# h stored whole and split in the third stage, reciprocal halves taken earlier, edge tiles placed earlier: a graph layer kernel on one core

## The chip, the cores and the metric

The kernel runs on one core of a Trainium2 chip. Its time is the device time of one launch in microseconds (us): a median of three runs, and beside it one execution that the hardware profiler recorded. The engines are TensorE (PE, its weight loads PEld), VectorE (DVE), ScalarE (ACT), GpSimd (POOL), and SyncE (SP), which here only issues transfers.

## The reference, cut to what matters

```python
def sage(x, W_l, W_r, b):                       # both layers use the same edges
    summed = segment_sum(x[src], dst, 10000)    # 10000 edges, 512 columns
    agg = summed / maximum(deg, 1)[:, None]
    return agg @ W_l.T + x @ W_r.T + b
xn = layernorm(x)                               # x: 10000 x 512
h = tanh(sage(xn, W1_l, W1_r, b1))
x = x + sage(h, W2_l, W2_r, b2) + linear_attention(xn)   # 8 heads, 64 features each
x = x + top1_of_8_experts(layernorm(x))
```

The linear attention needs, for each node and head, the query features times one shared matrix, divided by a denominator (the features times the sum of the keys' features). All matrix products are done as three products of halves: every operand is split into a high part, rounded to fp32r, and a low part, the full value minus the high one.

## The kernel before

The nodes are padded to 20 groups of 4 tiles of 128 nodes, 80 tiles. There are four stages, and each engine runs its own instruction stream; semaphores alone order them. The streams are written as loops over "steps": a function is called with `turn, k` for step t = 8 turn + k, and it works on tile t minus a lag that differs from one operation to the next (`active(t, lag, NT)`).

Stage 1 normalises the nodes and sums the keys. Stage 2 (`hidden`) computes h group by group: DVE adds the root part (`low`, L1031), ACT takes tanh and casts the high half (L836), DVE subtracts for the low half (`hT_made_low`), PE multiplies the halves with W2_l into y. SP loads the next group's `r_in` and `b_agg`, stores both halves of h to DRAM (L556) and y to `y_d`.

Stage 3 (`mix`) has one step for each tile. In step t:

- PE: in each fourth step the denominators of a group (L1315, 8 matmuls), then one matmul that spreads the inverse denominators of tile t-2 over its features (L1326), two matmuls that sum an edge tile (L417, L418), and 24 matmuls (L1200) for tile t-8, 12 of them with `hT_high` and `hT_low`, 12 with `qz_high` and `qz_low`.
- DVE: query features times the spread inverse of tile t-3 (`low<-phi_q,bank`, L1043), the build of one edge tile (`Sj`, `S`, `cnt`, `eidx`, L397 to L406), the addition of the product of tile t-9 to x (`m_x`, L1053), the low half `qz_low` of tile t-4; in each fourth step the reciprocal of the denominators (L1063), and in the step after it that reciprocal's low half (`z_halves`).
- ACT: the high half of the edge sources (`G_high`), in each fourth step that of the reciprocal (`z_halves`, L849), that of qz, and the copy of an edge sum to `O`.
- POOL: the low half of edge sources (`G_low`), the gather of an edge tile from `y_d` (L361), and the scatter of another (L378), which adds the rows `O` to `agg_d` in DRAM. The scatters are a chain: each waits until the one before it has landed (L377), since two could touch one row. The build of edge tile i waits until the scatter of tile i-4 has landed, and so does, by way of `G_low` behind the scatter in POOL's stream, the sum of tile i.
- SP: for each group the two halves of h (L593), the edge lists (L354), the store of a finished part (`part_d`, L597), x (`m_x`, L601) and query features (`phi_q`, L605), 1 MB each but for the lists.

An edge tile goes through its own steps s: gather at s, build and split at s+2, sum at s+3, scatter at s+4. The table `mix_edges` sets which s are done in which t: before, none for t below 6 and one in each step from there on, so that s = t-6, and the last sum is in step 88, one step after the last product (step 87). Stage 4 (`ffn`) begins when all scatters have landed: SP loads `agg2_g[0]` and `part_d[0]`, DVE makes x, its statistics and the normalised rows of four tiles, and PE transposes them (L1207).

Of the kernel before, what the change touches and what calls it, by code (L numbers as in the profile page):

```python
# [19 lines left out]
EDGE_FROM, EDGE_EXTRA = 6, 32  # L20
# [70 lines left out]
def build(nc, x, src, dst, w1lT, w1rT, b1, w2lT, w2rT, b2, wqT, wkT, wv, pmat, wproj, bproj,  # L91
          wr, br, f1, fb1, f2, fb2, ident_in, tri_in, bmask_in, hmask_in, trash_in, expand_in,
          iota_in, out):
    with ExitStack() as ctx:
# [9 lines left out]
        hT_d = split_d("hT", [NG, P, KC * GROUP])  # L104
        w1l_d, w2r_d, f1_d, f2_d = (split_d(w, [P, KC * D]) for w in ("w1l", "w2r", "f1", "f2"))
        q_d = nc.dram_tensor("q_d", [NG, P, KC * GROUP], F32)
# [66 lines left out]
        mhT = [at("hT_high", 2, 2, F32R), at("hT_low", 16, 2, F32R)]  # L173
# [98 lines left out]
        m_den, m_z, m_zh, m_zl, m_zb = (sem(f"mix_{n}") for n in ("den", "z", "z_high", "z_low", "z_spread"))  # L272
        m_qz, m_qh, m_ql = sem("mix_qz"), sem("mix_qz_high"), sem("mix_qz_low")
# [51 lines left out]
        for t in range(32):  # L325
            now = 0 if t < EDGE_FROM else 1 + (t % 2 if EDGE_EXTRA <= t < 32 else 0)
            mix_edges.append([(s // 8, s % 8) for s in range(done, done + now)])
            done += now
# [136 lines left out]
        def _(sp):  # L465
# [80 lines left out]
            def hidden(turn, b):  # L546
                g = 2 * turn + b
                end = isinstance(g, int) and g == NG
                if active(g, 1, NG):
                    sp.wait_ge(b_hl, 4 * g)  # L550
                    if end:
                        sp.dma_start(flat(phq[1]), q_d[1]).then_inc(m_ph[1], 16)
                    if active(g, -1, NG):
                        hid_in(*lagged(turn, b, -1, 2))
                    for n in range(2):
                        sp.dma_start(hT_d[n][g - 1], flat(bhT[n])).then_inc(b_hst, 16)  # L556
                    if end:
                        sp.wait_ge(b_hst, 64)
                        for i in range(2):
                            for n in range(2):  # L560
                                sp.dma_start(flat(mhT[n], i), hT_d[n][i]).then_inc(m_ht[i], 16)
                        for i in range(2):
                            edge_load(sp, 1, 0, i)
                    sp.wait_ge(b_yo, 4 * g)
                    sp.dma_start(y_g[g - 1], flat(by, 1 - b)).then_inc(b_yst[1 - b], 16)
                if isinstance(g, int) and g == 2:
                    sp.wait_ge(c_ml, KC)
                    for n in range(2):
                        sp.dma_start(flat(W2r[n]), w2r_d[n][:]).then_inc(s_w2r, 16)
                if isinstance(g, int) and g == 3:  # L570
                    sp.dma_start(flat(phq[0]), q_d[0]).then_inc(m_ph[0], 16)
# [6 lines left out]
            sp.wait_ge(b_hst, 32 * NG)  # L578
# [6 lines left out]
            def mix(turn, k):  # L585
# [3 lines left out]
                if active(g, 1, NG) and j == 0 and not (first and g < 3):  # L589
                    turn1, b1_ = lagged(turn, b, 1, 2)  # L590
                    sp.wait_ge(m_p, 4 * (g - 2))
                    for n in range(2):
                        sp.dma_start(flat(mhT[n], b1_), hT_d[n][g - 1]).then_inc(m_ht[b1_], 16)  # L593
# [54 lines left out]
        def _(pool):  # L648
# [67 lines left out]
            turns(pool, mix, 11, head=4, last=1)  # L716
# [14 lines left out]
        def _(act):  # L731
# [82 lines left out]
            def hidden(turn, b):  # L814
# [12 lines left out]
                if active(g, 0, NG):  # L827
                    for o in range(KC):
# [3 lines left out]
                        if o == 0:  # L832
                            need(act, b_y, 4 * g)
                            need(act, b_hst, 32 * g)
# [5 lines left out]
            def mix(turn, k):  # L840
                t = 8 * turn + k
                edges = edge_steps(turn, k)
                for te in edges[0:1]:
                    edge_high(act, 1, *te)
                if active(t, 1, NT) and k % 4 == 1:
                    g = 2 * turn + k // 4
                    act.wait_ge(m_z, g + 1)
                    need(act, m_zb, 4 * g)
                    act.copy(zs[0:STACK, :], pd[0:STACK, :]).then_inc(m_zh, 1)  # L849
                if active(t, 3, NT):  # L850
# [3 lines left out]
                    act.copy(mqz[0][:, kk // 4, kk % 4, :], low[:, kk % 4, :]).then_inc(m_qh, 1)  # L854
                for te in edges[0:1]:
# [18 lines left out]
            turns(act, mix, 11, head=4, last=1, skip=5)  # L874
# [31 lines left out]
        def _(dve):  # L906
# [104 lines left out]
            def hidden(turn, b):  # L1011
# [15 lines left out]
                for o in range(KC):  # L1027
                    if o == 0:
                        dve.wait_ge(b_rin[b], 16 * (turn + 1))
                    dve.wait_ge(b_h, 4 * g + o + 1)  # L1030
# [5 lines left out]
            group_turns(dve, hidden, 0, head=2, last=1)  # L1036

            def mix(turn, k):
                t = 8 * turn + k
                if active(t, 3, NT):  # L1040
# [13 lines left out]
                if active(t, 4, NT):  # L1054
# [3 lines left out]
                             mqz[0][:, kk // 4, kk % 4, :]).then_inc(m_ql, 1)  # L1058
                if active(t, 0, NT) and k % 4 == 0:
# [4 lines left out]
                if active(t, 1, NT) and k % 4 == 1:  # L1064
                    g = 2 * turn + k // 4
                    dve.wait_ge(m_zh, g + 1)
                    low_half(dve, zs[LOW:STACK, :], pd[LOW:STACK, :], zs[LOW:STACK, :]).then_inc(m_zl, 1)
# [6 lines left out]
            turns(dve, mix, 11, head=4, last=1)  # L1074
# [104 lines left out]
        def _(pe):  # L1179
# [164 lines left out]
            def mix(turn, k):  # L1344
# [8 lines left out]
                if active(t, 8, NT):  # L1353
                    turn8, kk = lagged(turn, k, 8)
                    b8, j8 = kk // 4, kk % 4
                    if j8 == 0:
                        pe.wait_ge(m_ht[b8], 32 * (turn8 + 1))
# [11 lines left out]
            turns(pe, mix, 11, head=4, last=1, skip=6)  # L1369
# [121 lines left out]
```

## Time and profile before

| | before |
|---|---|
| median of three runs | 2760.31 us (2755.53 to 2762.66) |
| profiled execution | 2753.52 us, span 2751.7 us |
| PE busy in the span | 2612.7 us |
| DVE busy | 1805.8 us |
| POOL busy | 1068.0 us |
| stage 2, from the first to the last group | about 1019 to 1491 us of the span |
| stage 3, steps with an edge sum | 1530.75 to 2131.87 us |
| first transpose of stage 4 | 2163.83 us |

Times inside the span count from its start. Busy time of PE is that of pipelined matmuls, whose ends are modelled; the start of one to the start of the next is the better measure of pace. Spans on POOL are rough. "Idle 4.85 <-DMA agg_d" behind an instruction says that its engine stood still for 4.85 us and what ended that.

### The profile page before, as it was taken

The numbers are of one execution on the slowest core, as the hardware profiler recorded it, in microseconds if no ns is written. First come the engines' busy times: TensorE is split into PE (matmuls) and PEld (weight loads), VectorE is DVE, ScalarE is ACT, GpSimd is POOL, SyncE is SP. The second block draws the span as 40 slices with busy tenths as digits, with TensorE's granted clock in tenths as the row PEclk, the third lists the DMA queues.
The fourth block names the chain that finished last, engine by engine and source line by source line (L and its number), as shares of the span: only waits on it lengthen the run. The fifth ranks groups of instructions, "written<-read, shape, count | busy, mean of one in ns | idle before, by whom it ended". The sixth has DMA issues, their size and how long they took to land.

```text
span 2751.7 us, 35957 instructions
## 1 busy us (share of the span) xinstructions
PE 2612.7 (95%) x11712; PEld 2084.5 (76%) x11712; DVE 1805.8 (66%) x3628; ACT 990.4 (36%) x1725; POOL 1068.0 (39%) x1009
## 2 busy tenths in 40 slices
PE   5999999999999989999999999999999499999999
PEld 4788888888888868888886666776667377777777
DVE  5577777777777734444444567777775577777774
ACT  3455454444444424444443222222222123233232
POOL 5677776666666620000000545455555211111110
PEclk8999999999999999999999999999999799999999
DMA  9766675555555446665556688887886423232231
GB/s 368 241 178 195 171 203 143 146 126 145 141 135 148 122 147 250 232 220 217 223 222 244 186 267 238 252 260 231 249 252 160 164 103 127 92 133 96 100 129 46
DMA packets 140315, 502.52 MB, mean 183 GB/s; under 512 B 27288, under 2 KB 27800, under 8 KB 99776
## 3 DMA queue, kind: packets, MB, share of 16 engines
q1 hardware_dynamic: 104384, 417.15, 41.7%
q0 software_dynamic: 35840, 84.23, 16.4%
q8 instruction: 47, 0.77, 0.1%
q14 instruction: 44, 0.36, 0.0%
HBM read 261.60 MB, written 239.73 MB: 182 GB/s over the span
## 4 chain that ended last, share of the span: by engine, by line
PE 72%; DMA 17%; DVE 4%; issue 3%; SPq 2%; ACT 1%; POOL 1%; POOLq 0%; DVEq 0%; ACTq 0%
PE bank L1200 56%; DMA agg_d<-O,eidx 14%; PE bank L1251 8%; PE bank L1207 3%; DVE x2T_low L314 2%; PE bank L1415 1%; SPq L484 1%; PE bank L417 1%; PE bank L418 1%; PE bank L1315 1%; ACT f_relu L883 1%; DVE f_relu L1119 1%; PE bank L1383 1%; PE bank L1400 0%; DMA a_x<-in_x 0%
## 5 line engine op out<-in xcount | busy, mean ns | idle before, releaser
L378 POOL DMA_INDIRECT agg_d<-O,eidx x160 | 271.6, 1697 | 300.9 <-DMA agg_d<-O,eidx 218.3
L314 POOL TENSOR_TENSOR G_low<-G,G_high 128x512 fp32r<-128x512 f32 x160 | 253.7, 1585 | 169.3 <-ACT G_high L439 169.2
L361 POOL DMA_INDIRECT G<-y_d,esrc x80 | 96.4, 1205 | 527.4 <-DMA y_d<-b_y 514.3
L397 DVE SCALAR_TENSOR_TENSOR Sj<-erow,dstf,tri 128x128 f32<-128x128 int32 x160 | 154.9, 968 | 146.6 <-DMA agg_d<-O,eidx 138.4
L439 ACT CAST G_high<-G 128x512 fp32r<-128x512 f32 x160 | 99.4, 621 | 315.6 <-DVE G L957 173.2
L723 POOL TENSOR_SCALAR veps<-mv 128x1 f32<-128x1 f32 x80 | 26.9, 337 | 472.9 <-DVE mv L1092 472.9
L314 DVE TENSOR_TENSOR qz_low<-low,qz_high 128x512 fp32r<-128x512 f32 x80 | 171.1, 2138 | 0.1
L406 DVE SCALAR_TENSOR_TENSOR eidx<-cnt,todump,dstf 128x1 int32<-128x1 f32 x160 | 149.7, 936 | 7.6
L688 POOL TENSOR_TENSOR pd<-pd,low 128x512 f32<-128x512 f32 (+1 forms) x80 | 143.3, 1792 | 0.0
L314 POOL TENSOR_TENSOR a_xn_rows_low<-a_x,a_xn_rows_high 128x512 fp32r<-128x512 f32 x80 | 142.9, 1786 | 0.2 <-ACT a_xn_rows_high L752 0.2
L1031 DVE TENSOR_TENSOR low<-bank,r_in 128x512 f32<-128x512 f32 x80 | 55.3, 692 | 131.0 <-PE bank L1200 131.0
L1200 PE MATMUL bank<-Wk_high,xnT_high 128*128 128x512 f32 x320 | 128.6, 402 | 6.3 <-DVE xnT_low L314 6.3
L1200 PE MATMUL bank<-xnT_high,W1r_high 128*128 128x512 f32 x320 | 131.5, 411 | 0.0
L1200 PE MATMUL bank<-W2r_high,hT_high 128*128 128x512 f32 x320 | 131.1, 410 | 0.0
L1200 PE MATMUL bank<-W2r_low,hT_high 128*128 128x512 f32 x320 | 130.5, 408 | 0.0
L966 DVE SCALAR_TENSOR_TENSOR low<-bank,low 128x512 f32<-128x512 f32 x80 | 55.3, 692 | 113.5 <-ACT low L770 113.5
L314 DVE TENSOR_TENSOR a_phi_low<-low,a_phi_high 128x512 fp32r<-128x512 f32 x80 | 59.9, 749 | 105.8 <-ACT a_phi_high L747 100.2
L1200 PE MATMUL bank<-W2r_high,hT_low 128*128 128x512 f32 x320 | 129.0, 403 | 0.0
L854 ACT CAST qz_high<-low 128x512 fp32r<-128x512 f32 x80 | 49.5, 619 | 218.2 <-PE bank L1200 148.0
L1200 PE MATMUL bank<-Wk_low,xnT_high 128*128 128x512 f32 x320 | 127.8, 399 | 0.0
L1200 PE MATMUL bank<-xnT_high,Wq_high 128*128 128x512 f32 x320 | 124.7, 390 | 2.5 <-DVE xnT_low L314 1.5
L1200 PE MATMUL bank<-Wk_high,xnT_low 128*128 128x512 f32 x320 | 127.0, 397 | 0.0
(199 smaller groups left out, 7872.0 us busy)
## 6 DMA issues: line engine op xcount, KB each, us to landing
agg_d<-zero SPq DMA_DIRECT2D x20, 1040.0 KB, 20.3
b_agg<-agg_d SPq DMA_DIRECT2D x20, 1040.0 KB, 8.5
a_x<-in_x SPq DMA_DIRECT2D x20, 1024.0 KB
agg_d<-z_halves SPq DMA_DIRECT2D x20, 1024.0 KB
q_d<-q_rows SPq DMA_DIRECT2D x80, 256.0 KB
r_d<-r_rows SPq DMA_DIRECT2D x80, 256.0 KB
r_in<-r_d SPq DMA_DIRECT2D x20, 1024.0 KB, 4.8
hT_high_d<-hT_made_high SPq DMA_DIRECT2D x20, 1024.0 KB, 10.4
```

Source lines behind the costliest of these rows:

```text
L314: return eng.tensor_tensor(out_, full, high.bitcast(F32), ALU.subtract)
L361: pool.indirect_dma_start(G[:, j, :], None, table, bass.IndirectOffsetOnAxis(ap=esrc[:, b, j:j + 1], axis=0)).then_inc(e_g[j], 16)
L378: pool.indirect_dma_start(agg, bass.IndirectOffsetOnAxis(ap=eidx[:, j, 0:1], axis=0), O[:, j, 0:width], None, compute_op=ALU.add).then_inc ...
L397: dve.scalar_tensor_tensor(Sj[:, :], row, dstf[:, b, j:j + 1], tri[:, :], ALU.is_equal, ALU.mult, accum_out=cnt[:, j:j + 1]).then_inc(e_cn ...
L406: dve.scalar_tensor_tensor(eidx[:, j, :], cnt1[:, j:j + 1], todump[:, b, j:j + 1], dstf[:, b, j:j + 1], ALU.mult, ALU.add).then_inc(e_s, 1)
L439: act.copy(G_high[:, j % 2, :], G[:, j, :]).then_inc(e_gh, 1)
L688: pool.tensor_tensor(acc[0:rows, :], acc[0:rows, :], low[0:rows, k % 4, :], ALU.add).then_inc(a_ks, 1)
L966: dve.scalar_tensor_tensor(lo, bank[7][:, :], 0.0, lo, ALU.max, ALU.add).then_inc(a_phi, 1)
L1031: dve.tensor_tensor(low[:, o, :], bank[2 + o % 2][:, :], rin[:, b, o, :], ALU.add).then_inc(b_hs, 1)
L1200: last = pe.matmul(out_, lhs(l, c), rhs(r, c), start=start and c == 0 and i == 0, stop=stop and c == KC - 1 and i == 2)
L1207: last = pe.transpose(psum[:, c * P:(c + 1) * P], row[:, c * P:(c + 1) * P], ident[:, :])
L1251: last = pe.matmul(bank[c][:, :], axr[l][:, 0, k5 % 4, c * P:(c + 1) * P], aph[r][:, k5 % 2, :], start=first and i == 0, stop=final and i ...
```

## The change

1. h is stored once, whole (1 MB a group instead of 2), from DVE's and ACT's working buffer `low`; this store is issued ahead of the loads of the next group. In stage 3 it is loaded once (1 MB instead of 2) into the place of `hT_low`; ACT then casts the high half and DVE subtracts for the low half, tile by tile, in step t for tile t-4, four steps ahead of the product. The load is still issued when the product of the group three back has been done, for its place is that of the old low half.
2. The reciprocal's high half on ACT now stands ahead of the high half of the edge sources, and its low half on DVE stands first in its step instead of last.
3. In steps 11, 15, 19, 23, 27 and 31 two edge tiles are done, the second behind the product. From step 32 on s = t: the last sum is in step 82, the last scatter in step 83.
4. The edge sources' low half stays on POOL (`edge_low` is not touched).

```diff
-EDGE_FROM, EDGE_EXTRA = 6, 32
...
-        hT_d = split_d("hT", [NG, P, KC * GROUP])
+        hT_d = nc.dram_tensor("hT_d", [NG, P, KC * GROUP], F32)
...
-        mhT = [at("hT_high", 2, 2, F32R), at("hT_low", 16, 2, F32R)]
+        mhT, hT = [at("hT_high", 16, 2, F32R), at("hT_low", 2, 2, F32R)], at("hT", 2, 2)
...
-            now = 0 if t < EDGE_FROM else 1 + (t % 2 if EDGE_EXTRA <= t < 32 else 0)
+            now = 0 if t < 6 else 1 + (t >= 8 and t % 4 == 3)
...
                     sp.wait_ge(b_hl, 4 * g)
+                    sp.dma_start(hT_d[g - 1], low[:, :, :].rearrange("p c n -> p (c n)")).then_inc(b_hst, 16)
                     if end:
                         sp.dma_start(flat(phq[1]), q_d[1]).then_inc(m_ph[1], 16)
                     if active(g, -1, NG):
                         hid_in(*lagged(turn, b, -1, 2))
-                    for n in range(2):
-                        sp.dma_start(hT_d[n][g - 1], flat(bhT[n])).then_inc(b_hst, 16)
...
                     sp.wait_ge(m_p, 4 * (g - 2))
-                    for n in range(2):
-                        sp.dma_start(flat(mhT[n], b1_), hT_d[n][g - 1]).then_inc(m_ht[b1_], 16)
+                    sp.dma_start(flat(hT, b1_), hT_d[g - 1]).then_inc(m_ht[b1_], 16)
...
-                for te in edges[0:1]:
-                    edge_high(act, 1, *te)
                 if active(t, 1, NT) and k % 4 == 1:
...
                     act.copy(zs[0:STACK, :], pd[0:STACK, :]).then_inc(m_zh, 1)
+                for te in edges[0:1]:
+                    edge_high(act, 1, *te)
...
+                if active(t, 4, NT):
+                    turn4, kk = lagged(turn, k, 4)
+                    if kk % 4 == 0:
+                        act.wait_ge(m_ht[kk // 4], 16 * (turn4 + 1))
+                    act.copy(mhT[0][:, kk // 4, kk % 4, :], hT[:, kk // 4, kk % 4, :]).then_inc(m_hh, 1)
...
                         dve.wait_ge(b_rin[b], 16 * (turn + 1))
+                        need(dve, b_hst, 16 * g)
...
+                if active(t, 1, NT) and k % 4 == 1:
+                    g = 2 * turn + k // 4
+                    dve.wait_ge(m_zh, g + 1)
+                    low_half(dve, zs[LOW:STACK, :], pd[LOW:STACK, :], zs[LOW:STACK, :]).then_inc(m_zl, 1)
...
+                    dve.wait_ge(m_hh, t - 3)
+                    low_half(dve, mhT[1][:, kk // 4, kk % 4, :], hT[:, kk // 4, kk % 4, :],
+                             mhT[0][:, kk // 4, kk % 4, :]).then_inc(m_hl, 1)
...
-                        pe.wait_ge(m_ht[b8], 32 * (turn8 + 1))
+                        pe.wait_ge(m_hl, t - 8 + 4)
```

DVE's stream in stage 3 of the program before, from the end of the step that takes a reciprocal into the step after it (`m_x` is the addition of a product, `low<-phi_q,bank` the query features times the spread inverse, the four rows between them the build of an edge tile):

```order
L1053 TENSOR_TENSOR m_x<-bank,m_x 128x512 [waits mix_product]
L314 TENSOR_TENSOR qz_low<-low,qz_high 128x512 [waits mix_qz_high]
L1063 RECIPROCAL pd<-bank 40x512 [waits mix_z_low,mix_den]
L1043 TENSOR_TENSOR low<-phi_q_96,bank 128x512 [waits mix_z_spread]
L397 SCALAR_TENSOR_TENSOR Sj,cnt<-erow,dstf,tri 128x128 [waits edge_scattered,edge_summed]
L399 TENSOR_SCALAR S,O<-erow,dstf 128x128
L402 TENSOR_SCALAR cnt<-cnt 128x1 [waits edge_repeats]
L406 SCALAR_TENSOR_TENSOR eidx<-cnt,todump,dstf 128x1 [waits edge_repeated]
L1053 TENSOR_TENSOR m_x<-bank,m_x 128x512 [waits mix_product,mix_x_in1]
L314 TENSOR_TENSOR qz_low<-low,qz_high 128x512 [waits mix_qz_high]
L314 TENSOR_TENSOR z_halves<-pd,z_halves 8x512 [waits mix_z_high]
```

The same place of the changed program:

```order
L1060 TENSOR_TENSOR m_x<-bank,m_x 128x512 [waits mix_product]
L314 TENSOR_TENSOR qz_low<-low,qz_high 128x512 [waits mix_qz_high]
L314 TENSOR_TENSOR hT_low<-hT,hT_high 128x512 [waits mix_h_high]
L1073 RECIPROCAL pd<-bank 40x512 [waits mix_z_low,mix_den]
L314 TENSOR_TENSOR z_halves<-pd,z_halves 8x512 [waits mix_z_high]
L1050 TENSOR_TENSOR low<-phi_q_97,bank 128x512 [waits mix_z_spread]
L397 SCALAR_TENSOR_TENSOR Sj,cnt<-erow,dstf,tri 128x128 [waits edge_scattered,edge_summed]
L399 TENSOR_SCALAR S,O<-erow,dstf 128x128
L402 TENSOR_SCALAR cnt<-cnt 128x1 [waits edge_repeats]
L406 SCALAR_TENSOR_TENSOR eidx<-cnt,todump,dstf 128x1 [waits edge_repeated]
L1060 TENSOR_TENSOR m_x<-bank,m_x 128x512 [waits mix_product]
```

Behind `qz_low` there is a new `hT_low` that waits for ACT, and the reciprocal stands behind it; the reciprocal's low half has moved from the end of the next step to its head.

SP's stream where stage 2 takes up its second and third group, before:

```order
L537 DMA r_in<-r_d 128x2048 [waits hid_h_low]
L538 DMA b_agg<-agg_d 128x2080
L556 DMA hT_high_d<-hT_made_high 128x2048
L556 DMA hT_low_d<-hT_made_low 128x2048
L565 DMA y_d<-b_y 128x2048 [waits hid_y_out]
```

and in the changed program:

```order
L551 DMA hT_d<-low 128x2048 [waits hid_h_low]
L537 DMA r_in<-r_d 128x2048
L538 DMA b_agg<-agg_d 128x2080
L563 DMA y_d<-b_y 128x2048 [waits hid_y_out]
L551 DMA hT_d<-low 128x2048 [waits hid_h_low]
```

One store now stands ahead of the two loads where two stores stood behind them.

## Rows read from the trace of the kernel before

**Rows 1.** Source line L378, 1490 to 2165 us: durations in ns, first and last start
```profile
L378 POOL DMA_INDIRECT agg_d<-O,eidx x80: 1552/1592/2097, 1539.5 to 2143.0; - x80
```

**Rows 2.** The chain that ended last: start us, us, what
```profile
1927.73 8.36 DMA agg_d<-O,eidx
1936.93 4.93 DMA agg_d<-O,eidx
1942.70 9.01 DMA agg_d<-O,eidx
1952.53 4.94 DMA agg_d<-O,eidx
```

**Rows 3.** Timeline of PE: the denominators of four groups, start us, us
```profile
1550.93 3.63 PE L1315 MATMUL bank<-phi_q,KS 128*40 128x512 f32 x8
...
1834.62 3.63 PE L1315 MATMUL bank<-phi_q,KS 128*40 128x512 f32 x8
1863.09 3.63 PE L1315 MATMUL bank<-phi_q,KS 128*40 128x512 f32 x8
...
2051.03 3.20 PE L1315 MATMUL bank<-phi_q,KS 128*40 128x512 f32 x7
```

**Rows 4.** What PE waited for, 1490 to 2165 us: us, times, longest
```profile
PE bank L1207 <- DVE f_xn L1098: 32.0, 1, 32.0
PE bank L1326 <- DVE z_halves L314: 22.7, 11, 3.8
PE bank L417 <- POOL G_low L314: 12.1, 5, 5.0
```

**Rows 5.** Timeline of SP: transfers that it issued in stage 3
```profile
1834.87 0.33 SPq L593 DMA_DIRECT2D hT_high<-hT_high_d  x1
...
1838.04 0.35 SPq L597 DMA_DIRECT2D part_d<-m_x  x1
...
2094.01 0.33 SPq L601 DMA_DIRECT2D m_x<-in_x  x1
```

**Rows 6.** Timeline of POOL: two scatters in a row late in stage 3
```profile
2096.72 1.59 POOL L378 DMA_INDIRECT agg_d<-O,eidx  x1 [1.43 <-ACT O L427]
...
2104.25 1.59 POOL L378 DMA_INDIRECT agg_d<-O,eidx  x1 [3.17 <-DMA agg_d<-O,eidx]
```

**Rows 7.** The DMA view, issues of stage 2: KB each, median us to landing
```profile
hT_high_d<-hT_made_high SPq DMA_DIRECT2D x18, 1024.0 KB, 10.4
hT_low_d<-hT_made_low SPq DMA_DIRECT2D x18, 1024.0 KB, 12.3
```

**Rows 8.** Timeline of DVE in stage 2, one group
```profile
1260.73 0.17 DVE L1002 TENSOR_SCALAR rd<-b_agg 128x4 f32<-128x4 f32 x1 [6.66 <-DMA b_agg<-agg_d]
...
1264.30 0.69 DVE L1031 TENSOR_TENSOR low<-bank,r_in 128x512 f32<-128x512 f32 x1 [1.30 <-PE bank L1200]
```

**Rows 9.** Timeline of the engines in stage 3: DVE and POOL side by side
```profile
1937.84 2.56 DVE L314 TENSOR_TENSOR qz_low<-low,qz_high 128x512 fp32r<-128x512 f32 x1
1937.98 1.86 POOL L314 TENSOR_TENSOR G_low<-G,G_high 128x512 fp32r<-128x512 f32 x1
1940.43 0.68 DVE L314 TENSOR_TENSOR z_halves<-pd,z_halves 8x512 fp32r<-8x512 f32 x1
```

**Rows 10.** Windows of stage 3: length, busy us of PE, PEld, DVE, ACT, POOL; clock, DMA share
```profile
1900.00:2000.00 100.00, 93.77 (x369) 69.01 (x369) 79.64 (x131) 24.00 (x43) 54.04 (x39) 0.97 0.83 242
```

**Rows 11.** From stage 3 to stage 4: first the chain, then DVE's timeline
```profile
2143.03 4.75 DMA agg_d<-O,eidx
2148.21 8.38 DMA f_x<-part_d
...
2156.61 0.17 DVE L1085 COPY rd<-rdeg 128x4 f32<-128x4 f32 x1 [24.49 <-DMA f_x<-part_d]
```

**Rows 12.** Timeline of PE: the last sum of stage 3, the first transposes of stage 4
```profile
2131.23 0.40 PE L417 MATMUL bank<-G_high,S 128*128 128x512 f32 x1
2163.83 2.58 PE L1207 MATMUL bank<-ident,f_xn 128*128 128x128 f32 x11 [31.96 <-DVE f_xn L1098]
```

More of the change, by code:

```diff
@@ L272, in build @@
         m_den, m_z, m_zh, m_zl, m_zb = (sem(f"mix_{n}") for n in ("den", "z", "z_high", "z_low", "z_spread"))
+        m_hh, m_hl = sem("mix_h_high"), sem("mix_h_low")
         m_qz, m_qh, m_ql = sem("mix_qz"), sem("mix_qz_high"), sem("mix_qz_low")
@@ L554, in hidden @@
                         hid_in(*lagged(turn, b, -1, 2))
-                    for n in range(2):
-                        sp.dma_start(hT_d[n][g - 1], flat(bhT[n])).then_inc(b_hst, 16)
                     if end:
-                        sp.wait_ge(b_hst, 64)
+                        sp.wait_ge(b_hst, 32)
                         for i in range(2):
-                            for n in range(2):
-                                sp.dma_start(flat(mhT[n], i), hT_d[n][i]).then_inc(m_ht[i], 16)
+                            sp.dma_start(flat(hT, i), hT_d[i]).then_inc(m_ht[i], 16)
                         for i in range(2):
@@ L577, in _ @@
                 sp.dma_start(flat(mx_, b), x_g[b]).then_inc(m_x[b], 16)
-            sp.wait_ge(b_hst, 32 * NG)
+            sp.wait_ge(b_hst, 16 * NG)
             sp.dma_start(craw[:, 0, 0:KC * EXP].rearrange("p (c e) -> p c e", c=KC), kpn(wr)
@@ L591, in mix @@
                     sp.wait_ge(m_p, 4 * (g - 2))
-                    for n in range(2):
-                        sp.dma_start(flat(mhT[n], b1_), hT_d[n][g - 1]).then_inc(m_ht[b1_], 16)
+                    sp.dma_start(flat(hT, b1_), hT_d[g - 1]).then_inc(m_ht[b1_], 16)
                 if j == 1:
@@ L715, in mix @@
                                            ALU.mult).then_inc(s_zf, 1)
-            turns(pool, mix, 11, head=4, last=1)
+            turns(pool, mix, 6, head=4, last=1)
             pool.wait_ge(e_sc, 16 * 2 * NT)
@@ L873, in _ @@
                     mix(0, k)
-            turns(act, mix, 11, head=4, last=1, skip=5)
+            turns(act, mix, 6, head=4, last=1, skip=5)
             act.wait_ge(s_zf, 4)
@@ L1036, in _ @@
             group_turns(dve, hidden, 0, head=2, last=1)
+            dve.wait_ge(b_hst, 16 * NG)
             def mix(turn, k):
                 t = 8 * turn + k
+                if active(t, 1, NT) and k % 4 == 1:
+                    g = 2 * turn + k // 4
+                    dve.wait_ge(m_zh, g + 1)
+                    low_half(dve, zs[LOW:STACK, :], pd[LOW:STACK, :], zs[LOW:STACK, :]).then_inc(m_zl, 1)
                 if active(t, 3, NT):
@@ L1063, in mix @@
                     dve.reciprocal(pd[0:STACK, :], bank[2][0:STACK, :]).then_inc(m_z, 1)
[L1064 to L1067, printed above, removed]
                 if isinstance(t, int) and t == 17:
@@ L1073, in mix @@
                     low_half(dve, high, craw[LOW:STACK, 1, :], high).then_inc(s_csp, 1)
-            turns(dve, mix, 11, head=4, last=1)
+            turns(dve, mix, 9, head=4, last=1)
             def pre(turn, k, j):
@@ L1368, in mix @@
                     edge_pe(pe, 1, *te, bank[7][:, :])
-            turns(pe, mix, 11, head=4, last=1, skip=6)
+            turns(pe, mix, 8, head=4, last=1, skip=6)
             pe.wait_ge(s_csp, 5)
```

1 line of the change is left out of this document (removed).

## The prediction

> **What bounds the kernel now.** The third stage is the one that the change rewrites, so I read it first. The source view of the scatters [rows 1] shows 80 of them, starting between 1539.5 and 2143.0 us: 79 intervals of 7.64 us on average, 30.6 us for the four of a group. The chain that ended last says what an interval is made of [rows 2]: from 1936.93 a scatter takes 4.93 us to land and the next starts 5.77 us after it; from 1927.73 and 1942.70 landing takes 8.36 and 9.01 us, and the intervals are 9.20 and 9.83 us. In each case the next scatter starts about 0.8 us behind the landing: the chain is bound by its own landings. The four intervals of a group are two short ones and two long ones, 5.77 x 2 + 9.20 + 9.83 = 30.6 us, the mean again.
>
> PE's own pace is in the denominators of successive groups [rows 3]: 1834.62 to 1863.09 is a group in which PE hardly stood still, 28.47 us. Sixteen groups took from 1550.93 to 2051.03, 500.1 us, where 16 x 28.47 = 455.5. So PE loses 44.6 us in them, and the scatters at 30.6 us a group are what paces the stage. The waits of PE [rows 4] show where this surfaces: 12.1 us for `G_low`, which stands behind a scatter in POOL's stream, and 22.7 us for `z_halves`, which on DVE stands behind an edge build that waits for a landing. The third entry, 32.0 us, is the passage to stage 4.
>
> The long intervals go with SP's loads [rows 5]: a group has one burst of both halves of h and a part's store (from 1834.87), and one of `m_x` and `phi_q`. Everything over the short pace is 603.5 - 79 x 5.77 = 148 us, about 8 a group, 4 for each burst.
>
> **The change, part by part.**
>
> *One MB of h less to load per group.* 18 loads of stage 3 fall away. What one costs the chain is not shown directly. The nearest row is the lone `m_x` load at 2094.01 [rows 5]: the interval of the scatter issued after it, 2096.72 to 2104.25, is 7.53 us [rows 6], 1.76 over 5.77. From the other side: in rows 2 the long interval at the h burst (three transfers) is 9.20 and that at the other burst (two) 9.83, so the third transfer may cost nothing. Ends 0 and 1.8; I take 1.6, near the lone load, because a load of the same kind and size is measured there, while the two bursts differ in phase and in having a store. 18 x 1.6 = -29 us, with -32 and 0 as ends.
>
> The Trainium skill says (DMA: Bandwidth & Descriptors, Queues, rings and completion order) that each DMA engine takes turns between the queues, a packet at a time. By this rule a scatter that is wholly inside a burst is no faster when the burst is shorter, and this term tends to 0. Rows 2 agree in so far as the longer burst gives no longer interval; rows 6 show that even one load slows a scatter.
>
> *Edges six steps earlier.* Before, the last sum starts at 2131.23 and stage 4's first transposes at 2163.83, 32.6 us later [rows 12]. In that time the last scatters land (2143.03 + 4.75), `part_d` is loaded in 8.38 us, and DVE works from 2156.61, 7.2 us [rows 11]. Afterwards the last sum stands in step 82, with six products still to come. A group is 28.47, of which 3.63 are denominators and some 0.4 around them; a step is 6.1, without its three single matmuls 5.5 us. Six are 33; landing and loads (11.8 + 4.75 + 8.4 = 25) hide below them. Then 1 us for the last addition and 7.2 us of DVE: 41.4 us from last sum to transposes, 9 more than before, if the chain paces both. The stall of 32.0 us in rows 4 becomes some 8, but products move into it. Against this, the last sum can now lie further ahead of its scatter: a sum must wait for the scatter three items back to start, then 1.05 us to `G_low` and its 1.86 [rows 2, 9], so it can lead its own scatter by three intervals less 3: 14.3 us with short ones, 18 with a long one, against 11.8 now. That gives back 4. Net +5 us.
>
> The double steps themselves add no scatter: in steps 11 to 31 a group needs five instead of four, 5 x 5.77 + 6.4 = 35 us against PE's 29, so PE waits there, and has 5.5 us a step less to wait for later. In a sum paced by the chain this is already counted.
>
> *Casting and subtracting h.* ACT gets 80 casts; it is busy 24.00 of 100 us [rows 10], so they are hidden there. DVE gets 80 subtractions. Their price lies between 0.68 and 2.56 us [rows 9]: `qz_low` starts while `G_low` runs on POOL and ends 0.6 us behind it, while `z_halves`, also two operands from SBUF, right behind `qz_low`, with POOL issuing a gather, takes 0.68. The new `hT_low` stands exactly where that `z_halves` stood. I take 0.68. DVE is busy 79.64 of 100 us, 24.3 a group of 30.5; with 4 x 0.68 it is 27.0, under the new chain pace of 29.0. The cover is thin: 2 us a group.
>
> The Trainium skill (SBUF — State Buffer, Who interferes with whom) has it that a DVE instruction with two SBUF inputs and a GpSimd instruction that reads SBUF exclude each other for their whole length. The trace agrees, 2.56 against 0.68; if that held for the new subtraction each time, DVE would pace the stage (third rival).
>
> The load of h is now needed in the step in which it is issued. The path from it: load at most 8.4 us, taking the one that shared its queue in rows 11, cast 0.6, subtraction 0.7, reciprocal 3.3, its halves 1.3: 14.3 us and 0.3 to issue. PE needs it for the spread two steps on, after 4.0 + 2 x 6.1 = 16.2 us. It fits with 1.6 us. ACT's edge copy waits behind the cast; it has a whole step. For the tightness of both I add 1.5 us.
>
> *Reciprocal's low half first.* The 22.7 us of rows 4 go, but where the chain paces, PE then waits for `G_low` instead: 0 in this sum, more if the chain is freed.
>
> *Stage 2.* The store now lies ahead of the loads. One MB of store is worth 12.3 + 0.45 (issued later) - 10.4 = 2.35 us of the queue [rows 7]. DVE waits 6.66 us for `b_agg` and then stands idle 1.30 for PE [rows 8]; two banks let the addition come one product (2.75, half of 5.5) less its own 0.7 and some 0.3 later still, in all 3.0 us of room. 2.4 fit. A few groups land later: +1 us, with 0 and +8 as ends. At the end of stage 2 the store stands ahead of the `phi_q` load for which PE waits: +2.4 us. The new wait of DVE on the store itself has a store issued 13 us earlier: nothing.
>
> **Sum.** -29 + 5 + 1.5 + 0 + 1 + 2.4 = -19 us. The profiled execution was 2753.5, which gives 2734.4. It lies 6.8 below the median of the runs shown; on that I say 2741 us.
>
> **Rivals.**
>
> 1. *The chain is freed and PE paces.* If a load costs over 2.1 us a group, the chain falls to PE's 28.5. Then PE gets back its 44.6 us and, at the end, 32.6 - 8.2 = 24; the five groups with five scatters cost 5 x (35 - 28.5) less 10 us that sums may run ahead, +23; with stage 2 and the store 3.4: -42, 2718 us. For it: the lone load's 1.76 is near. Against: the bursts of rows 2.
> 2. *No relief.* By the packet rule worked out on rows 2, the term is 0 and the rest stays: +10, 2770 us, slower. It decides at 18p = 10, p = 0.55 us a load. For it: 9.20 against 9.83. Against: rows 6.
> 3. *DVE paces.* If `hT_low` takes over 1.2 us on average, 24.3 + 4p is over 29.0. At 2.56 each group is 34.5, 5.5 more in the 12 groups behind step 32: +66 on the forecast, 2807 us. For it: DVE's shift against `G_low` changes. Against: only one `G_low` of 1.86 runs per edge tile, and `qz_low` or another already pays for it.
>
> **How the numbers follow.** Forecast 0.48 (its own range 2728 to 2752), first rival 0.19, second 0.19, third 0.14, with its smaller forms near 2765 to 2790. The range is 2712 to 2774: about 0.08 lie below, 0.11 above. 0.3% is 8.3 us, about what a measurement of this kernel can tell from no change: faster is under 2752, 0.45 + 0.19 + 0.02 = 0.66; the same 0.03 + 0.10 + 0.04 = 0.17; slower 0.17.
>
> **What the profile would show.** Right: 80 scatters, the mean interval down from 7.64 to about 7.3 us, the long one at h's burst near 7.6 while the other keeps 9; four-step groups of about 35 us before step 32 and 29 behind it; no wait of PE for `z_halves` and a wait for `f_xn` of about 8 instead of 32; `hT_low` at 0.7; stage 2 groups unchanged. Wrong: both long intervals as before (second rival), groups at 28.5 (first), `hT_low` or `qz_low` beyond 2 us together over 3.3 and DVE over 95% busy (third), or stage 2 groups longer by over 0.5 us, as the store's place would do it.

## The result, and the profile after

The changed kernel takes 2736.01 us (median of 4 runs, 2733.61 to 2737.19) against 2758.15 us before (4 runs), a ratio of 0.9917 with a 95% interval of 0.99 to 0.9934. Its profiled execution took 2733.61 us, span 2731.8 us; before it was 2753.52 and 2751.7. The forecast was 2741.

I read the same views as before, in the same order. First the source view of the scatters from 1490 to 2165 us, durations in ns and first and last start, as in [rows 1]:

```profile
L378 POOL DMA_INDIRECT agg_d<-O,eidx x80: 1552/1591/2104, 1544.2 to 2109.4; - x80
```

The 79 intervals now take 565.2 us, 7.15 each, where [rows 1] gave 603.5 and 7.64. That is 38.3 us less. The first scatter is 4.7 us later than before. PE's timeline, the denominators of six of the 20 groups, start and length:

```profile
1555.40 3.63 PE L1321 MATMUL bank<-phi_q,KS 128*40 128x512 f32 x8
1592.45 3.63 PE L1321 MATMUL bank<-phi_q,KS 128*40 128x512 f32 x8
...
1741.03 5.32 PE L1321 MATMUL bank<-phi_q,KS 128*40 128x512 f32 x8
...
1942.54 3.63 PE L1321 MATMUL bank<-phi_q,KS 128*40 128x512 f32 x8
1971.00 3.63 PE L1321 MATMUL bank<-phi_q,KS 128*40 128x512 f32 x8
...
2056.40 3.63 PE L1321 MATMUL bank<-phi_q,KS 128*40 128x512 f32 x8
```

Two regimes are to be seen. The five groups from 1555.40 to 1741.03, which have five edge tiles each, take 37.1 us each. The eleven behind them take 28.67 on average, and 1942.54 to 1971.00 is the 28.5 us of a PE that hardly waits: there the scatters pace no more. All sixteen together take 501.0 us, against 500.1 in [rows 3]. So seen from PE these groups gained nothing; what was won behind step 32 was spent ahead of it. The gain sits in the passage. PE's waits from 1490 to 2165 us, the five largest:

```profile
PE bank L417 <- POOL G_low L314: 15.0, 7, 3.8
PE bank L1332 <- DVE low L1050: 8.8, 5, 4.7
PE bank L1213 <- DVE f_xn L1104: 7.9, 1, 7.9
PE bank L417 <- DVE eidx L406: 6.9, 5, 2.1
PE bank L1321 <- DVE pd L1073: 4.9, 1, 4.9
```

The 32.0 us for `f_xn` of [rows 4] are 7.9, and the 22.7 for `z_halves` are gone. PE's timeline at the passage, the last sum and stage 4's first transposes as in [rows 12]:

```profile
2098.96 0.40 PE L417 MATMUL bank<-G_high,S 128*128 128x512 f32 x1
...
2140.13 3.64 PE L1213 MATMUL bank<-ident,f_xn 128*128 128x128 f32 x16 [7.86 <-DVE f_xn L1104]
```

The transposes start 23.7 us earlier than before. That is 4.7 (first scatter later) - 38.3 (chain) + 9.9 (from the last scatter to the transposes 30.7 us, before 20.8). Stage 4 then took 591.7 us in this execution and 587.9 in that of before: PE waits twice for `f_relu`, 2.8 us in all, behind DVE gaps that no other engine explains. The kernels below took 589 to 595 there, so I count this as a difference between executions.

Last, DVE, by the tile views of `qz_low` and of the new `hT_low` (min/median/max ns), and its timeline at the head of stage 3 and in one group of stage 2:

```profile
L314 DVE TENSOR_TENSOR qz_low<-low,qz_high x80: 673/682/2648, 1505.7 to 2105.7; 128x512 fp32r<-128x512 f32 x80
L314 DVE TENSOR_TENSOR hT_low<-hT,hT_high x80: 677/689/2845, 1508.9 to 2106.3; 128x512 fp32r<-128x512 f32 x80
```

```profile
1261.89 0.17 DVE L1003 TENSOR_SCALAR rd<-b_agg 128x4 f32<-128x4 f32 x1 [7.67 <-DMA b_agg<-agg_d]
...
1264.44 0.69 DVE L1033 TENSOR_TENSOR low<-bank,r_in 128x512 f32<-128x512 f32 x1 [0.28 <-PE bank L1206]
...
1492.29 3.35 DVE L1073 RECIPROCAL pd<-bank 40x512 f32<-40x512 f32 x1 [5.04 <-DMA hT_d<-low]
```

`qz_low`, 2.56 us in [rows 9] and 2.53 in the median of all 80 before, has a median of 0.68, and `hT_low` one of 0.69. In stage 2 the wait for `b_agg` grew by 1.0 us and the idle time for PE shrank by as much, from 1.30 to 0.28: hidden. At the head of stage 3 there is a wait that was not there, 5.04 us for the last store of h.

### The profile page after: what moved, and what is told of

Read it like the earlier page. It is cut to its first block, busy times and chain, and to the rows that moved or that the text cites. A ratio compares the mean times of both kernels' runs of the same rounds, so it can differ in the third digit from the quotient of the medians.

```text
span 2731.8 us, 36032 instructions
## 1 busy us (share of the span) xinstructions
PE 2612.9 (96%) x11712; PEld 2081.5 (76%) x11712; DVE 1836.8 (67%) x3708; ACT 1031.0 (38%) x1805; POOL 1061.6 (39%) x1009
## 4 chain that ended last, share of the span: by engine, by line
PE 82%; DMA 7%; DVE 5%; SPq 2%; issue 2%; ACT 2%; POOL 1%; POOLq 0%; DVEq 0%; ACTq 0%
PE bank L1206 63%; PE bank L1257 8%; DMA agg_d<-O,eidx 5%; PE bank L1213 3%; PE bank L1321 2%; DVE x2T_low L314 2%; PE bank L1421 1%; PE bank L417 1%; PE bank L418 1%; SPq L484 1%; DVE f_relu L1125 1%; PE bank L1332 1%; ACT f_relu L884 1%; SPq L486 1%; PE bank L1406 1%
## 5 line engine op out<-in xcount | busy, mean ns | idle before, releaser
L378 POOL DMA_INDIRECT agg_d<-O,eidx x160 | 275.4, 1721 | 234.6 <-DMA agg_d<-O,eidx 165.7
L314 POOL TENSOR_TENSOR G_low<-G,G_high 128x512 fp32r<-128x512 f32 x160 | 244.0, 1525 | 209.0 <-ACT G_high L439 209.0
L361 POOL DMA_INDIRECT G<-y_d,esrc x80 | 87.2, 1090 | 529.8 <-DMA y_d<-b_y 516.9
L397 DVE SCALAR_TENSOR_TENSOR Sj<-erow,dstf,tri 128x128 f32<-128x128 int32 x160 | 188.7, 1179 | 55.4 <-DMA agg_d<-O,eidx 55.3
L406 DVE SCALAR_TENSOR_TENSOR eidx<-cnt,todump,dstf 128x1 int32<-128x1 f32 x160 | 139.7, 873 | 7.6
L1206 PE MATMUL bank<-aggT_high,W1l_high 128*128 128x512 f32 x320 | 125.5, 392 | 1.5 <-DVE aggT_low L314 1.5
L1206 PE MATMUL bank<-x2T_high,F_high 128*128 128x512 f32 x320 | 126.9, 397 | 0.0
```

The costliest lines, as they stand in the source:

```text
L314: return eng.tensor_tensor(out_, full, high.bitcast(F32), ALU.subtract)
L361: pool.indirect_dma_start(G[:, j, :], None, table, bass.IndirectOffsetOnAxis(ap=esrc[:, b, j:j + 1], axis=0)).then_inc(e_g[j], 16)
L378: pool.indirect_dma_start(agg, bass.IndirectOffsetOnAxis(ap=eidx[:, j, 0:1], axis=0), O[:, j, 0:width], None, compute_op=ALU.add).then_inc ...
L397: dve.scalar_tensor_tensor(Sj[:, :], row, dstf[:, b, j:j + 1], tri[:, :], ALU.is_equal, ALU.mult, accum_out=cnt[:, j:j + 1]).then_inc(e_cn ...
L406: dve.scalar_tensor_tensor(eidx[:, j, :], cnt1[:, j:j + 1], todump[:, b, j:j + 1], dstf[:, b, j:j + 1], ALU.mult, ALU.add).then_inc(e_s, 1)
L1206: last = pe.matmul(out_, lhs(l, c), rhs(r, c), start=start and c == 0 and i == 0, stop=stop and c == KC - 1 and i == 2)
```

## The experiments

All ratios are to the kernel before, with 95% intervals. "Transposes" is the start of stage 4's first ones; it was 2163.8 before and 2140.1 in the changed kernel. Each ratio is to runs of before that were taken with that experiment, so a difference between two changed kernels is given both by the medians and by the ratios. The diffs are cut; `...` marks what is left out, and where the edge table changes, the number of steps behind each engine's loop follows it.

**e1, the table of edge steps alone.**

```diff
-            now = 0 if t < EDGE_FROM else 1 + (t % 2 if EDGE_EXTRA <= t < 32 else 0)
+            now = 0 if t < 6 else 1 + (t >= 8 and t % 4 == 3)
```

> The kernel before with the new table of edge steps alone: two edge tiles in steps 11, 15, ..., 31, and s = t from step 32. Theory A (the chain of scatters paces, and the load of one MB less is what shortened it): the chain stays at 7.64 us an interval, its last scatter is near 1544 + 603 = 2147 us, and the passage to stage 4 costs 10 us more than before since six products still stand behind the last sum: +5 to +14 us on before. Theory B (the earlier place of the edges is what gained, since the landings and the load of the part now hide below six products, 24 of the 32 us stall): faster than before by 15 to 24 us, nearly all of the change's gain.

Measured: 2788.04 us, ratio 1.011 (1.0095 to 1.0126), 31 us slower by the medians. Theory B is out, and A saw too little. The profiled execution (2778.10, the shortest of the four by 9 us) has the transposes at 2185.0, 21 us late. Its source view of the scatters and its waits of PE:

```profile
L378 POOL DMA_INDIRECT agg_d<-O,eidx x80: 1552/1591/2105, 1538.0 to 2159.0; - x80
```

```profile
PE bank L1326 <- DVE z_halves L314: 48.9, 19, 4.1
```

The intervals grew from 7.64 to 7.86 us, and the wait for `z_halves` from 22.7 to 48.9. DVE waited 176.7 us for landings at `Sj` (before 138.4), and `z_halves` stands behind it in the same step. Behind step 32 one interval in each group is 10 to 12.6 us long. That these waits feed each other is how I read it; e6 tests it.

**e2, h whole alone.** The changed kernel with the old table and the old places of the reciprocal's halves:

```diff
-            now = 0 if t < 6 else 1 + (t >= 8 and t % 4 == 3)
+            now = 0 if t < 6 else 1
...
```

> The changed kernel with the table of edge steps and the place of the reciprocal's halves as before, so h stored whole, loaded once and split in stage 3 alone. Theory A (chain shortened by the load that is gone, 1.6 to 2.1 us a group): mean interval 7.2 to 7.3 us, -20 to -30 us on before, the wait of PE for f_xn still about 32 us. Theory B (the gain came from the edges' place): within 5 us of before. Theory C (both are needed: each lets the other work): about half of the 22 us.

Measured: 2727.81 us, 0.9897 (0.9881 to 0.9913), 29 us faster than before and 6 to 8 faster than the whole change, whose interval overlaps with this one. Theory A by the number; e8 and e9 ask for its cause. The scatters and PE's waits, and `qz_low`:

```profile
L378 POOL DMA_INDIRECT agg_d<-O,eidx x80: 1552/1591/2072, 1541.2 to 2106.2; - x80
```

```profile
PE bank L1213 <- DVE f_xn L1104: 29.8, 1, 29.8
PE bank L1332 <- DVE z_halves L314: 13.1, 11, 5.9
```

```profile
L314 DVE TENSOR_TENSOR qz_low<-low,qz_high x80: 673/682/2661, 1505.3 to 2068.0; 128x512 fp32r<-128x512 f32 x80
```

The chain is 565.0 us, the same 7.15 an interval as with all parts, and the stall at the passage stays. So this part alone gives the whole shortening of the chain.

**e3, the reciprocal's halves alone.**

```diff
+                if active(t, 1, NT) and k % 4 == 1:
+                    act.copy(zs[0:STACK, :], pd[0:STACK, :]).then_inc(m_zh, 1)
                 for te in edges[0:1]:
                     edge_high(act, 1, *te)
...
+                    low_half(dve, zs[LOW:STACK, :], pd[LOW:STACK, :], zs[LOW:STACK, :]).then_inc(m_zl, 1)
                 if active(t, 3, NT):
...
```

The same lines go from their old places.

> The kernel before with the reciprocal's halves ahead of the edges alone, on ACT and DVE. Theory A (the chain paces): PE's 22.7 us for z_halves vanish and turn up as waits for G_low or for the edge build; time within 3 us of before. Rival: those waits were on the path, and up to 22 us are gained. Second rival: the half ahead of the edge build delays the build, each fourth sum and scatter comes 1 us later: +10 to +20 us.

Measured: 2751.59 us, 0.9981 (0.9967 to 0.9994), 5 us faster. PE's wait for `z_halves` vanished from its trace and that for `G_low` rose from 12.1 to 23.0 us, as theory A has it; the time lies a little beyond the 3 us it allowed, and the second rival is out.

**e4, four steps with two edge tiles instead of six.**

```diff
-            now = 0 if t < 6 else 1 + (t >= 8 and t % 4 == 3)
+            now = 0 if t < 6 else 1 + (12 <= t < 28 and t % 4 == 3)
```

> The changed kernel with four steps of two edge tiles (15, 19, 23, 27) instead of six, so that s = t - 2 behind them. Of after the trace shows 37.1 us for a group with five tiles and 28.5 for one with four, and the last scatter lands some 10 us earlier than it must. Theory PE (PE paces wherever there are four): two groups shorter by 7.5 to 8.6 us, the end 2 us later: -13 to -15 us on the changed kernel, about 2722. Theory chain (80 scatters at their own pace set the time, wherever they stand): within 3 us of the changed kernel, 2736.

Measured: 2729.55 us, 0.9888 (0.9873 to 0.9904), 6 to 8 us under the changed kernel. That is between the two theories; the intervals of the ratios just overlap, so this run alone proves little.

**e5, h whole and the halves, with the old table.** The line of e2 in the changed kernel, with the ends of the loops that go with it; the halves keep their new places.

> The changed kernel with one edge tile a step and s = t - 6 as before: h whole and the reciprocal's halves ahead, no new table. Theory A (the parts add up: -28 for h alone, -5 for the halves alone): about -33 us on before, 2724, so the table costs the changed kernel 12 us. Theory PE: with h whole the groups are at 28.5 to 29.4 us, so PE nearly paces, and the halves' 13.1 us of waits come back in part: 2718 to 2724. Rival: the halves cost as much as they save, since the new low half of h stands on the same engine: 2728, as with h alone. Mean interval of the scatters 7.1 us, wait for f_xn still 30 us.

Measured: 2722.30 us, 0.988 (0.9865 to 0.9895): 34 us faster than before, 10 to 14 faster than the change. The parts add up. PE's timeline, the fourth and the last denominators, and the passage:

```profile
1556.51 3.63 PE L1321 MATMUL bank<-phi_q,KS 128*40 128x512 f32 x8
...
2011.98 3.63 PE L1321 MATMUL bank<-phi_q,KS 128*40 128x512 f32 x8
...
2091.30 0.40 PE L417 MATMUL bank<-G_high,S 128*128 128x512 f32 x1
...
2123.59 2.79 PE L1213 MATMUL bank<-ident,f_xn 128*128 128x128 f32 x12 [31.64 <-DVE f_xn L1104]
```

Sixteen groups in 455.5 us, that is 28.47 each: PE at its own pace in every one. The stall of 31.6 us is there in full, and the kernel is faster all the same.

**e6, h whole and the table, the halves in their old places.** The edit of e3, taken back in the changed kernel.

> The changed kernel with the reciprocal's halves in their old places, so h whole and the new table. Theory loop (with s = t the edge build that waits for a landing stands ahead of the low half for which PE waits, and PE's delay comes back to the next sum): 10 to 25 us slower than the changed kernel, 2746 to 2760, waits for z_halves over 25 us, and one scatter interval of 11 us in each group, as in the run of the table alone. Theory sum (each part for itself): the halves were worth 5 us, 2741.

Measured: 2740.53 us, 0.9941 (0.9927 to 0.9954): 5 to 7 us above the changed kernel, as theory sum has it; the two intervals touch, so more than the size can't be said. Waits for `z_halves` were 29.6 us, but they cost little; the loop of e1 is weak once h is loaded whole.

**e7, two steps with two edge tiles.**

```diff
-            now = 0 if t < 6 else 1 + (t >= 8 and t % 4 == 3)
+            now = 0 if t < 6 else 1 + (t in (15, 23))
```

> The changed kernel with two steps of two edge tiles (15 and 23), s = t - 4 behind them. Theory floor (80 scatters at 7.1 us and 21 us from the last to stage 4 set the time wherever the edges stand; more than four products behind the last sum only add to the end): 2718 to 2724, a few us under four doubles and as without any. Theory PE: each double costs a PE-paced group 7 to 8 us and saves at most a step of the 30 us at the end: 2720 to 2724, with f_xn waited for some 18 to 20 us.

Measured: 2730.73 us, 0.9892 (0.9873 to 0.991), with runs from 2717.85 to 2738.14. Both theories expected 2718 to 2724, and it is no better than four; with such a spread the run decides nothing between them. The profiled execution (2738.14) is the longest of them and waits 20.3 us for `f_xn`, as expected.

**e8, before, with one of two halves loaded.**

```diff
-                    for n in range(2):
-                        sp.dma_start(flat(mhT[n], b1_), hT_d[n][g - 1]).then_inc(m_ht[b1_], 16)
+                    sp.dma_start(flat(mhT[0], b1_), hT_d[0][g - 1]).then_inc(m_ht[b1_], 16)
...
-                        pe.wait_ge(m_ht[b8], 32 * (turn8 + 1))
+                        pe.wait_ge(m_ht[b8], 16 * (turn8 + 2))
```

> The kernel before, but stage 3 loads only the high half of h from the third group on; the low half keeps what it held, so the output is not the reference's. It leaves out 18 loads of 1 MB and adds no work. Theory A (a load of 1 MB costs the chain of landings 1.6 to 2.1 us): mean interval 7.64 to 7.15-7.28, -29 to -38 us. Theory packets (a scatter inside a burst is no faster when the burst is shorter): within 5 us of before; then the gain of h stored whole would come from the stores of stage 2 or from the order of SP's stream.

Measured: 2741.48 us, 0.9948 (0.9934 to 0.9962), 14.6 us faster. The interval fell to 7.36:

```profile
L378 POOL DMA_INDIRECT agg_d<-O,eidx x80: 1552/1592/2097, 1542.0 to 2123.6; - x80
```

The chain took 581.6 us, 21.9 less than before, so a load costs it about 21.9 / 18 = 1.2 us. Theory packets is out, theory A has the sign and half the time. Half of what h whole gains is thus not shown to be the load.

**e9, h whole, with casts and subtractions left out.**

```diff
-                    act.copy(mhT[0][:, kk // 4, kk % 4, :], hT[:, kk // 4, kk % 4, :]).then_inc(m_hh, 1)
+                    if isinstance(t, int) and t < 12:
+                        act.copy(mhT[0][:, kk // 4, kk % 4, :], hT[:, kk // 4, kk % 4, :]).then_inc(m_hh, 1)
...
-                    low_half(dve, mhT[1][:, kk // 4, kk % 4, :], hT[:, kk // 4, kk % 4, :],
-                             mhT[0][:, kk // 4, kk % 4, :]).then_inc(m_hl, 1)
+                    if isinstance(t, int) and t < 12:
+                        low_half(dve, mhT[1][:, kk // 4, kk % 4, :], hT[:, kk // 4, kk % 4, :],
+                                 mhT[0][:, kk // 4, kk % 4, :]).then_inc(m_hl, 1)
...
```

In what is left out here, the wait for the load moves from ACT to PE, and PE takes `hT` itself in place of its low half.

> The kernel of h whole alone, with the casts on ACT and the subtractions on DVE left out behind the first two groups (PE then multiplies a stale high half and the whole h, so the output is not the reference's). Loads, stores and PE's work are those of h whole alone. Theory bytes (what h whole gains beyond the 15 us of one load less comes from the stores of stage 2 and the shorter start of stage 3): 2724 to 2729, mean interval 7.1 to 7.2 us. Theory timing (the added instructions shift DVE's stream, so that qz_low no longer runs beside G_low and the transfers of a group are issued further apart): without them qz_low is at 2.5 us again, the interval back at 7.3 to 7.4 us, 2738 to 2743.

Measured: 2744.27 us, 0.9953 (0.9936 to 0.997). With 144 instructions less it is about 16 us slower than e2, the intervals of the two apart, so theory bytes is out. Scatters and `qz_low`:

```profile
L378 POOL DMA_INDIRECT agg_d<-O,eidx x80: 1553/1592/2096, 1544.3 to 2119.3; - x80
L314 DVE TENSOR_TENSOR qz_low<-low,qz_high x80: 672/2536/3601, 1507.6 to 2081.2; 128x512 fp32r<-128x512 f32 x80
```

The interval is back at 7.28 and `qz_low` at a median of 2.54 us, both as theory timing has it.

**e10, before, with a sixteenth of each half loaded.**

```diff
-                        sp.dma_start(flat(mhT[n], b1_), hT_d[n][g - 1]).then_inc(m_ht[b1_], 16)
+                        sp.dma_start(flat(mhT[n], b1_)[:, 0:128], hT_d[n][g - 1][:, 0:128]).then_inc(m_ht[b1_], 16)
```

> The kernel before, but from the third group on stage 3 loads only a sixteenth of each half of h (64 KB instead of 1 MB); the rest of the halves is stale, so the output is not the reference's. Theory linear (each MB in stage 3 costs the chain of landings about the same): a second MB less gives another 12 to 20 us on the 15 of the first, until PE paces at 7.12 us an interval: 2722 to 2730. Theory packets (only the presence of a burst counts, and the part's store still makes one): near the 2741 us of one half loaded.

Measured: 2703.11 us, 0.9802 (0.978 to 0.9824), below what either theory allowed. Of the 2 MB that before loads, 1/8 MB is left. Against e8, with 1 MB, that is 38 us for 7/8 MB where the first MB gave 15: more than linear. The scatters:

```profile
L378 POOL DMA_INDIRECT agg_d<-O,eidx x80: 1552/1591/1992, 1541.3 to 2094.1; - x80
```

7.00 us an interval, and PE's groups are at 28.5 throughout. `qz_low` has a median of 0.68 us here too. DVE's and ACT's streams are those of before, so less to load can by itself keep `qz_low` away from `G_low`, and the two effects are not apart in this run.

**e11, e5 with the load of the part ahead.**

```diff
-            sp.wait_ge(e_sc, 16 * 2 * NT)
-            sp.dma_start(flat(fa[0]), agg2_g[0]).then_inc(f_a[0], 16)
             sp.wait_ge(m_qz, NT)
             sp.dma_start(flat(fx[0]), part_d[0]).then_inc(f_p[0], 16)
+            sp.wait_ge(e_sc, 16 * 2 * NT)
+            sp.dma_start(flat(fa[0]), agg2_g[0]).then_inc(f_a[0], 16)
```

> h whole and the reciprocal's halves ahead, without the new table (2722 us), and at the passage to stage 4 the load of the part issued before the wait for the last scatter, ahead of that of the sums. Before, the second of the two loads landed 8.4 us after its issue, and DVE waited for it. Theory queue: a 1 MB load alone lands 4.6 to 5.5 us after its issue, so the 31.6 us wait for f_xn falls by 2.5 to 4 us and the kernel to about 2719. Rival: the landing of the last scatters is slowed by the load beside them, or the load of the sums lands as late by itself: within 1 us.

Measured: 2720.19 us, 0.9873 (0.9847 to 0.9899), 2 us under e5, which the intervals don't tell from nothing, so neither theory is decided by the time. SP's and DVE's timelines show the effect at its place:

```profile
2110.33 0.33 SPq L618 DMA_DIRECT2D f_xn<-agg_d  x1
...
2117.02 0.17 DVE L1091 COPY rd<-rdeg 128x4 f32<-128x4 f32 x1 [22.41 <-DMA f_xn<-agg_d]
```

6.7 us from issue to DVE. In e5 the pair was issued at 2107.38 and DVE began at 2116.36, 9.0 us. From the last scatter to the transposes it is 18.6 instead of 20.7, and the wait for `f_xn` is 29.9 us instead of 31.6, less than theory queue had.

**e12, the changed kernel with a step for each transfer.** The load of `m_x` moves from `j == 1` to `j == 3` of its group:

```diff
-                    if active(g, 1, NG) and not (first and g < 3):
+                if j == 3 and active(g, 1, NG) and not (first and g < 3):
...
```

> The changed kernel with the load of m_x moved from the second to the fourth step of its group, so that h, the part's store, phi_q and m_x have a step each. Theory bursts (a scatter beside two transfers is slowed more than two beside one each): the groups with five scatters, which the chain paces, fall from 37.1 to 35 or 36 us, 5 to 10 us in all, about 2728. Theory bytes (only the bytes that go through in a group count): within 3 us of the changed kernel.

Measured: 2747.01 us, 0.9964 (0.995 to 0.9978), 11 to 13 us slower than the changed kernel. Both theories are out as to the time. The scatters:

```profile
L378 POOL DMA_INDIRECT agg_d<-O,eidx x80: 1552/1592/2090, 1543.2 to 2118.8; - x80
```

That is 7.29 us an interval, with `qz_low` at a median of 0.68. PE's denominators start at 1554.33 us where the five groups with five tiles begin, at 1736.59 behind them and at 2063.90 last. So these groups did fall, from 37.1 to 36.5 us, part of what theory bursts had; but the eleven behind them rose from 28.67 to 29.76, 12 us in all, and that is the loss.

## Why the prediction came out

The time was right, 2741 against 2736, and the direction. That is in part luck: two terms were too small, with opposite signs, and made up for each other, so I go through them.

*One MB of h less: -29 forecast.* Alone, h whole gave -29 (e2), but my sum for it was -24, for it added 1.5 for the split, 1 for stage 2 and 2.4 for SP's queue. What the step named, the load, is worth 15 us (e8), within the ends -32 and 0 and half of the value taken: this is the term that was mis-sized. The other half comes with the split, priced at +1.5, which turned out to be worth -16 (e9 against e2). Why is not settled. It is shown that the instructions and their waits do it, with the same transfers, and that `qz_low` falls from 2.5 to 0.7 us with them, since it seldom runs beside `G_low` then; e12 has the short `qz_low` too and an interval of 7.29, so that alone doesn't make the pace. Nor did the transfers' spacing, at least as e12 spread them. The traces show the place: in each group between 1590 and 2045 us I take the longest scatter interval that touches the stretch from 1 to 6 us behind the issue of h's load. Its mean is 10.0 us before, 10.1 in e8 and 9.8 in e9, but 8.3 in e2, 7.8 in e5 and 6.8 in e10. The same at the load of `m_x` is 8.4 to 9.9 in all six. Each is one execution, but by them one load less alone did not shorten the interval at h's burst that the prediction had in view; with the split it did.

*Edges six steps earlier: +5 forecast.* Measured +10 to +14 beside h whole (e6 against e2, the change against e5) and +31 without it (e1). The path from the last sum to the transposes was priced at 41.4 us (its terms add up to 41.2) and took 41.2. What failed is the 4 us that were to come back because sums can run ahead: the last sum leads its scatter by 10.4 us, not by 14.3 or more, and before by 11.8. And "in a sum paced by the chain this is already counted" failed, for with h whole PE paces and not the chain. A group with five tiles takes 37.1 us, not 35. There 25 scatters start between 1560 and 1741 us, 7.25 us apart, so five take 36.3. PE's own work was slower too: the granted clock was 0.93 on average from 1560 to 1740 us in the changed kernel, where PE was busy for 154 of the 180 us, and 1.00, its upper level of 2.4 GHz, in e5, where it was busy for all 180. How much of the 37.1 is the clock is not shown. In e5 PE paces at 28.47 us a group, so against it each of the five costs 8.7: with the eleven others the last denominators are 2056.40 - 2011.98 = 44.4 us later. For that the last sum stands six steps further ahead, which brings back less than it cost: it starts at 2098.96 instead of 2091.30, 7.7 later. Then the way from it to the transposes is 41.2 instead of 32.3 us, 8.9 more. Together these are the 16.5 us by which the transposes are later than in e5.

*The rest.* The halves were put at 0 and gave 5 us (e3; e5 against e2 the same). Stage 2 was put at +1 and shows 0, its wait just covered as worked out: PE's first denominators start at 1484.31 us, before at 1484.17. At the head of stage 3 the sum had 1.5 + 2.4 us; the first scatter is 4.7 late. But the cause I had ruled out takes part: the new wait on the store of h, "issued 13 us earlier: nothing", holds only inside stage 2. At its end DVE waits 5.04 us for the store that was issued last. What it costs is not shown: in e2, with the same wait, the first scatter is 1.7 us late, and in e8 and e10, which have no such wait, 2.5 and 1.8.

*The rivals.* No relief (0.19) is out by e8 and e10. For it stood a rule of the Trainium skill (DMA: Bandwidth & Descriptors, Queues, rings and completion order), that each DMA engine takes turns between queues packet by packet; these runs don't contradict the turns, but what I drew from them, that a shorter burst helps no scatter, is wrong here: the mean interval is 7.64, 7.36 and 7.00 us with two, one and a sixteenth of two loads. DVE paces (0.14) is out: `hT_low` has a median of 0.69 us and DVE was busy 83.67 of the 100 us of [rows 10]. The first rival (0.19), that the chain is freed and PE paces, is what the trace shows behind step 32, and in e5 everywhere. Its condition, over 2.1 us a group, is met only by load and split together: the chain of e2 is 38.5 us shorter, 2.1 a group, that of e8 1.2. Its 2718 took the groups with five tiles as 5 x 6.5 - 10; with the measured 5 x (37.1 - 28.5) = 43 it would have said 2753.5 - 44.6 - 24 + 43 + 3.4 = 2731 for the profiled execution, which took 2733.6. So the likeliest case had the number and the first rival the mechanism in the main.

The signs I had named: no wait for `z_halves`, 8 us for `f_xn`, `hT_low` at 0.7 and stage 2 unchanged all came, and of the two long intervals, taken as above in the changed kernel, h's is 7.7 us (forecast 7.6) and that at `m_x` 8.3 (forecast 9). The mean interval of 7.15 instead of 7.3 and groups of 28.5 instead of 29 were the first rival's.

The best kernels here that do all the work are e5 and e11, 2722 and 2720 us: the change without its table. e10 is faster but leaves most of h unloaded.

## What to carry to other kernels

A shorter stall at a passage is worth nothing by itself: here the new table took it from 32 to 8 us, and the kernel lost 10 to 14. Moving work ahead of it pays only if the resource that paces has room where the work goes; so price each moved item at the chain's own interval, not at the engine's, and ask again what paces once the other parts of the change are in. And where a chain depends on landings, an edit of a few instructions can move it by as much as a megabyte: test the parts of a change one by one, for they may have opposite signs.

## What the runs showed of the hardware

Leaving out casts and subtractions behind the second group made the kernel 16 us slower (2744.27 against 2727.81), with the same transfers. A DVE subtraction of 128x512 from two SBUF operands, `qz_low`, takes 0.68 us or about 2.5 us with little between (median 2.53 to 2.54 us before, in e8 and in e9; 0.68 in the change, in e2, e10 and e12), and which of the two depends on what POOL runs beside it. Before, 62 of the 80 took over 2.3 us, and each of them shares at least 1.7 us with a `G_low` of POOL; the 18 short ones share 0.5 us at most. In the changed kernel 18 are long, each with a `G_low` beside it. The Trainium skill says such a pair excludes each other (SBUF — State Buffer, Who interferes with whom), and the two levels agree with that; it can't say which instruction will meet which. Another 7/8 MB less to load per group gave 38 us after the first MB gave 15 (e10, e8). One 1 MB load took 9.0 us from its issue to the waiting engine as the second of a pair; with the pair moved apart the load that was waited for took 6.7 us (e5, e11).
